# New written-out orders for the four compute engines in the third stage of a decoder kernel

## The reference, cut to what matters

```python
x = x + experts(...)                       # the last addition of layer 0
x = x + windowed_attention(layernorm(x))   # 16 heads of 16, 4 key heads, rotary angles, a sink
x = x + attention_over_heads(layernorm(x), ctx)   # per token: 16 heads against 16 heads
# gated feed-forward with a low-rank modulation taken from one more attention
z = layernorm(x); attn = causal_attention(rmsnorm(z))
mod = 0.1 * tanh(attn @ A); h = rmsnorm(z)
gate = silu(h @ W_in.T + mod * (h @ A) @ B)
x = x + z + (gate * (h @ W_up.T)) @ W_down.T
```

## Time and profile before

| | us |
|---|---|
| three runs | 3188.6, 3181.32, 3175.71 (median 3181.32) |
| the profiled execution | 3189.76, its span 3187.0 |
| mean granted clock of TensorE in it | 0.942 |
| third stage in it | about 2050 to 3187 |
| rounds in which all letters work | about 2234 to 2995 |

### The profile page before, as it was taken

The page is one execution under the profiler, slowest core; times in us unless marked ns, Lnnn a source line. Parts: engine busy times, 40 slices in busy tenths (PEclk is TensorE's granted clock), DMA queues, the critical chain, the costliest instruction groups (busy, mean ns, idle before and its releaser), DMA issues. The chain is left out here.

```text
span 3187.0 us, 68763 instructions
## 1 busy us (share of the span) xinstructions
PE 2848.2 (89%) x21832; PEld 2312.8 (73%) x21864; DVE 2618.5 (82%) x5725; ACT 1953.1 (61%) x4213; POOL 2128.5 (67%) x2555
## 2 busy tenths in 40 slices
PE   6999999999999999997786799657899989999988
PEld 3888888888888888885443577435677777777767
DVE  6888888888888888886698566478999999999973
ACT  5888878777877878784332333245565656565542
POOL 5986666666666666665576200169999999999880
PEclk8999999999999999998887799767999999999989
DMA  4564444444444444443321222300000000000000
GB/s 144 174 205 148 143 146 128 145 136 138 142 139 131 151 128 136 147 139 119 104 86 62 85 77 77 122 14 17 20 18 26 18 26 18 26 18 26 19 5 10
DMA packets 178644, 288.04 MB, mean 90 GB/s; under 512 B 42256, under 2 KB 103833, under 8 KB 177708
## 3 DMA queue, kind: packets, MB, share of 16 engines
q1 hardware_dynamic: 172206, 267.46, 26.1%
q0 software_dynamic: 6144, 16.79, 1.6%
HBM read 221.99 MB, written 53.78 MB: 87 GB/s over the span
## 5 line engine op out<-in xcount | busy, mean ns | idle before, releaser
L1747 POOL TENSOR_TENSOR l_prod<-l_sco,l_kv 128x256 f32<-128x256 f32 x512 | 444.8, 908 | 41.1 <-DVE l_sco L2259 41.1
L1740 POOL TENSOR_TENSOR l_prod<-l_q,l_kv 128x256 f32<-128x256 f32 x512 | 358.8, 741 | 17.9 <-DVE l_att L2267 17.9
L717 DVE SCALAR_TENSOR_TENSOR a_cq<-a_PQ,a_taps,a_cq 128x504 f32<-128x504 f32 (+2 forms) x384 | 281.8, 734 | 74.2 <-ACT a_cq L583 65.1
L717 DVE SCALAR_TENSOR_TENSOR a_ck<-a_PK,a_taps,a_ck 128x504 f32<-128x504 f32 (+2 forms) x384 | 280.8, 731 | 10.0 <-ACT a_ck L583 0.9
L341 POOL TENSOR_TENSOR a_tq<-a_cq,a_tq 128x512 f32<-128x512 f32 x128 | 165.9, 1296 | 132.2 <-ACT a_tq L589 132.1
L328 POOL TENSOR_TENSOR a_hrs<-a_hve,a_neghalf 128x8 f32<-128x8 f32 x128 | 209.7, 1638 | 25.6 <-DVE a_hve L734 25.1
L484 PE MATMUL a_Y<-a_wo,a_og_parts 128*128 128x256 f32 x1536 | 206.2, 284 | 4.2 <-POOL a_og_parts L335 4.2
L411 PEld LDWEIGHTS a_X<-a_wv,a_xb 128*128 128x128 f32 x1536 | 199.9, 188 | 12.1 <-issue 1.2
L411 PE MATMUL a_PQ<-a_x_hi,a_wqk 128*128 (+1 forms) x512 | 195.6, 423 | 12.5 <-issue 11.8
L341 POOL TENSOR_TENSOR a_tk<-a_ck,a_tk 128x512 f32<-128x512 f32 x128 | 163.6, 1278 | 63.3 <-ACT a_tk L589 63.3
L411 PE MATMUL a_X<-a_wv,a_xb 128*128 128x256 f32 x1536 | 204.2, 282 | 0.8 <-DMA a_xb<-a_x_lo 0.8
(11 more groups left out here) (403 smaller groups left out, 8624.9 us busy)
## 6 DMA issues: line engine op xcount, KB each, us to landing
a_wqk<-qk_parts SPq DMA_DIRECT2D x112, 512.0 KB, 3.3
a_wv<-v_parts SPq DMA_DIRECT2D x56, 512.0 KB, 3.8
a_wg<-g_parts SPq DMA_DIRECT2D x112, 256.0 KB, 3.3
a_wo<-o_parts SPq DMA_DIRECT2D x112, 256.0 KB, 2.9
a_dr<-decays SPq DMA_DIRECT2D x256, 64.0 KB, 2.5
m_hs<-sorted_rows SPq DMA_DIRECT2D x72, 128.0 KB, 2.0
sorted_outs<-m_ys SPq DMA_DIRECT2D x72, 128.0 KB, 1.7
qk_parts<-a_wqk SPq DMA_DIRECT2D x16, 512.0 KB, 3.1
```

The lines of the kernel that those rows point to most:

```text
L717: nc.vector.scalar_tensor_tensor(out=acc, in0=src, scalar=taps[p][:, tap + k:tap + k + 1], in1=acc, op0=ALU.mult, op1=ALU.add).then_inc(s_ ...
L1740: nc.gpsimd.tensor_tensor(out=prod[:, h], in0=qv[:, h:h + 1, :].to_broadcast([P, H, HD]), in1=kk, op=ALU.mult).then_inc(S("E_pqk"), 1)
L1747: nc.gpsimd.tensor_tensor(out=prod[:, h], in0=sco[:, h:h + 1, :].to_broadcast([P, HD, H]), in1=vv, op=ALU.mult).then_inc(S("E_pav"), 1)
```

## The change

The order of the pieces is new on TensorE, ScalarE, VectorE and (one swap) GpSimd, in the third stage alone. SyncE's list is the same. No instruction is added, removed or altered, and the waits inside each piece are the same. Against its neighbours:

- TensorE: `e_xT` goes to the head of the round, `d_oT` and `d_wo` from behind `m_half(1)` to just behind `e_q`, `m_half(1)` from behind `f_zT` to behind `ft_av`, `d_s` before `f_v`, `d_v` behind `ft_a`.
- VectorE: `d_x` from behind the statistics of D to right behind `combine`, `m_hidden(0)` behind `d_x`, `f_x2lo` to just ahead of the last `et_values`, `ft_gm_lo` ahead of `arguments("D")`, other orders among the `et_scores` and the `et_values`, `split_low` before `et_x`.
- ScalarE: the copies follow TensorE's new order; `exponentials("F")` comes before the copies of D, `m_tanh(0)` behind `et_exp`, `normalise("E")` to the end of the round.
- GpSimd: the `power` of E before that of D.

```diff
--- before.py
+++ after.py
@@ -1760,7 +1760,7 @@
                                                  bass.IndirectOffsetOnAxis(ap=of_tile[:, k:k + 1], axis=0)).then_inc(S(f"G_in{k}"), 16)
 
             pool.wait_ge(S("const"), 16)
-            iterate(pool, [("F", power("F", 2)), ("Et", products_av), ("Dn", power("D", 1)), ("En", power("E", 1)), ("E", products_qk),
+            iterate(pool, [("F", power("F", 2)), ("Et", products_av), ("En", power("E", 1)), ("Dn", power("D", 1)), ("E", products_qk),
                            ("G", gather)])
 
         @block.tensor
@@ -1980,9 +1980,9 @@
                 last = product(MI[:, m * R:(m + 1) * R], lambda c: fwo[:, c, m * P:(m + 1) * P], lambda c: fa[:, c, :])
             last.then_inc(S("woa_p"), 1)
             pe.wait_ge(S("woa"), 1)
-            iterate(pe, [("M", m_half(0)), ("D", d_xT), ("E", e_xT), ("Dt", d_eT), ("D", d_qk), ("Dt", d_av), ("Ft", ft_eT), ("E", e_q),
-                         ("F", f_zT), ("M", m_half(1)), ("Ft", ft_av), ("Dt", d_oT), ("D", d_qkT), ("Dt", d_wo), ("F", f_qk),
-                         ("Ft", ft_oT), ("D", d_v), ("F", f_v), ("Ft", ft_a), ("D", d_s), ("Md", m_down), ("Et", et_aT), ("Et", et_wo),
+            iterate(pe, [("E", e_xT), ("M", m_half(0)), ("D", d_xT), ("Dt", d_eT), ("D", d_qk), ("Dt", d_av), ("Ft", ft_eT), ("E", e_q),
+                         ("Dt", d_oT), ("F", f_zT), ("Dt", d_wo), ("D", d_qkT), ("F", f_qk), ("Ft", ft_av), ("M", m_half(1)),
+                         ("Ft", ft_oT), ("D", d_s), ("F", f_v), ("Ft", ft_a), ("D", d_v), ("Md", m_down), ("Et", et_aT), ("Et", et_wo),
                          ("F", f_s)])
 
         @block.scalar
@@ -2139,14 +2139,14 @@
             act.wait_ge(S("woa_p"), 1)
             nc.scalar.activation(woa[:], MI[:, 0:DC * R].rearrange("p (c r) -> p c r", c=DC), ACT.Copy).then_inc(S("woa"), 1)
             act.wait_ge(S("const"), 16)
-            iterate(act, [("M", m_tanh(0)), ("D", leave(xT["D"], EB, "D_xTp", "D_pv", "D_xT")), ("Dt", weights_T("D", "F", -4)),
-                          ("Ft", exponentials("F")), ("E", leave(xTE, P1, "E_xTp", "E_qp", "E_xT")), ("Et", et_exp),
-                          ("F", normalise("F")), ("F", f_x2), ("F", f_x1), ("Ft", weights_T("F", "D", 5)), ("E", e_q), ("F", f_x2hi),
-                          ("M", m_tanh(1)), ("Dt", leave(oT["D"], EB, "D_oTp", "D_wo", "D_oT")), ("D", spread_keys("D", P1, "D_qkTp")),
-                          ("D", queries("D", P1, "D_qkTp", "D_q")), ("Ft", leave(oT["F"], MI, "F_oTp", "F_ap", "F_oT")),
-                          ("F", f_residual), ("F", spread_keys("F", P0, "F_pj")), ("Ft", ft_mod), ("D", d_vb), ("Ft", ft_gm_hi),
-                          ("En", normalise("E")), ("Et", leave(attT, EB, "E_aTp", "E_wo", "E_aT")),
-                          ("F", queries("F", P0, "F_pj", "F_qk")), ("Dn", normalise("D")), ("F", f_vb), ("Et", split_high),
+            iterate(act, [("E", leave(xTE, P1, "E_xTp", "E_qp", "E_xT")), ("Ft", exponentials("F")),
+                          ("D", leave(xT["D"], EB, "D_xTp", "D_pv", "D_xT")), ("Dt", weights_T("D", "F", -4)), ("Et", et_exp),
+                          ("M", m_tanh(0)), ("F", normalise("F")), ("E", e_q), ("Dt", leave(oT["D"], EB, "D_oTp", "D_wo", "D_oT")),
+                          ("F", f_x1), ("Ft", weights_T("F", "D", 5)), ("D", queries("D", P1, "D_qkTp", "D_q")), ("F", f_x2),
+                          ("D", spread_keys("D", P1, "D_qkTp")), ("F", queries("F", P0, "F_pj", "F_qk")),
+                          ("F", spread_keys("F", P0, "F_pj")), ("M", m_tanh(1)), ("Ft", leave(oT["F"], MI, "F_oTp", "F_ap", "F_oT")),
+                          ("F", f_residual), ("F", f_x2hi), ("Ft", ft_mod), ("Ft", ft_gm_hi), ("D", d_vb), ("Dn", normalise("D")),
+                          ("Et", leave(attT, EB, "E_aTp", "E_wo", "E_aT")), ("F", f_vb), ("Et", split_high), ("En", normalise("E")),
                           ("D", exponentials("D"))])
 
         @block.vector
@@ -2317,12 +2317,13 @@
 
             dve.wait_ge(S("d_in"), 16 * D_WEIGHTS)
             dve.wait_ge(S("const"), 16)
-            iterate(dve, [("Et", et_scores(0)), ("Ft", arguments("F")), ("F", statistics("F", "E_x", 1)), ("Et", et_scores(2)),
-                          ("Et", et_scores(1)), ("Et", et_scores(3)), ("Et", et_shift), ("Dt", divide("D", EB)), ("Et", et_weights),
-                          ("M", m_hidden(0)), ("D", d_rope), ("Dn", combine), ("Et", et_values(0)), ("Ft", divide("F", MI)),
-                          ("Dn", statistics("D", "G_x", 2)), ("F", f_x2lo), ("Dt", d_x), ("M", m_hidden(1)),
-                          ("En", statistics("E", "D_x", 1)), ("Et", et_values(2)), ("Et", et_values(1)), ("Ft", ft_gm),
-                          ("Et", et_values(3)), ("D", arguments("D")), ("Ft", ft_gm_lo), ("Md", m_x), ("Et", et_x), ("Et", split_low)])
+            iterate(dve, [("Et", et_scores(0)), ("Ft", arguments("F")), ("Et", et_scores(1)), ("Et", et_scores(2)),
+                          ("F", statistics("F", "E_x", 1)), ("Et", et_scores(3)), ("Et", et_shift), ("Dt", divide("D", EB)),
+                          ("Et", et_weights), ("D", d_rope), ("Dn", combine), ("Dt", d_x), ("M", m_hidden(0)),
+                          ("En", statistics("E", "D_x", 1)), ("Dn", statistics("D", "G_x", 2)), ("Ft", divide("F", MI)),
+                          ("Et", et_values(1)), ("M", m_hidden(1)), ("Et", et_values(2)), ("Et", et_values(0)), ("Ft", ft_gm),
+                          ("F", f_x2lo), ("Et", et_values(3)), ("Ft", ft_gm_lo), ("D", arguments("D")), ("Md", m_x), ("Et", split_low),
+                          ("Et", et_x)])
 
 
 def decoder(nc, a, x_in, out):
```

## The result

The changed kernel takes 3249.52 us (median of 4 runs, 3239.06 to 3256.48), the kernel before 3178.93 beside it (4 runs). The ratio is 1.0211, 95% interval [1.0183, 1.0239]: slower by 2.1%, outside the range. The profiled execution took 3249.72 us. Medians here are over all runs of a kernel; the ratios leave out runs that were disturbed as a whole.

A forecast was written before the change was run, and what follows sets the result against it. VectorE's list was taken to bound the kernel at 31.54 us a round. Terms +8.4 + 2.4 + 3.2 - 5.0 + 1.1 = +10.1 us, carried to the 3181.3 us median, gave 3191 us, range 3166 to 3209.

The forecast's parts named there:

- VectorE's order alone: VectorE's list in the third stage: only L2195 gets shorter, -0.22 us a round if VectorE stays the bound.
- term of the drain: Last round of `et_values`: `f_x2lo`, 5.81 us beside GpSimd's products, no longer holds up `m_hidden(1)`; -5.0 us.
- `arguments("D")` to `arguments("F")`: `f_s` starts 0.84 us later: no cost in full rounds, with 0.3 to spare; +2.4 us in the fill.
- `divide("D")` to `ft_gm`: Chain through TensorE grows to 14.71 us; VectorE waits 0.6 us a round, net 0.35 taken, +8.4 us over 24 rounds.
- L2195: VectorE instruction directly behind `et_weights`: 643 ns at the median before, expected near its least value, 424 ns.
- The fill and the drain: Ends of the stage: fill +2.4 us, drain -5.0 and +1.1 us, with L2289 under 1.5 us.
- The lowered clock: TensorE's time lost to the clock: half of 13.7 us reaches the end, +3.2 us; bounds -3.6 to +10.1.
- rival B: TensorE's clock falls behind several short stops in nearly every round: +27 us, 3208 us, granted clock under 0.96; chance 0.20.

The follow-up runs named there:

- e6: Kernel before with `ft_gm_lo` moved ahead of `arguments("D")`, nothing else; 3231.04 us, ratio 1.0162.
- e1: Changed kernel with `ft_gm_lo` put back behind `arguments("D")`; 3245.87 us, ratio 1.0179.
- e3: Changed kernel without L2214, the scale applied in ScalarE's exponential instead; 3243.94 us, ratio 1.0157.
- e11: Changed kernel with one more GpSimd wait, ahead of product 12 of 16, for the value L2214 writes; 3238.90 us, ratio 1.0166.
- e10: Changed kernel, L2214 kept, with GpSimd's gathers behind `power("F")` and waiting for `D_av` from the tenth tile on; 3251.32 us.
- e4: VectorE's list of the kernel before, with the new lists of TensorE, ScalarE and GpSimd; 3326.03 us, ratio 1.0436.
- e7: e3 with GpSimd's two gathers put behind `power("F")` and waiting for `D_av`; 3194.42 us, ratio 1.0032.
- e8: Kernel before without L2214 and with the gathers behind `power("F")`, waiting for `D_av`; 3194.13 us, ratio 1.0038.
- e9: e7 with the gathers moved only from the tenth tile on, at their old place before that; 3171.46 us, ratio 0.9951.
- e12: Kernel before without L2214 and with the gathers moved from the tenth tile on; 3174.65 us, ratio 0.9960.
- e2: Changed kernel with `statistics("F")` put back directly behind `arguments("F")`, ahead of `et_scores(1)` and (2); 3256.53 us, ratio 1.0206.

## Why the prediction was wrong

*The step that failed* is in "VectorE's order alone": "The others that work from SBUF alone beside GpSimd's products (`combine`, `f_x2lo`, `ft_gm_lo`) stay beside products, so I leave their times." L2214 is of that kind, and I did not even list it. The earlier trace rows had the price, 5.81 us in place of 0.87 for one arrival in a burst of products; I took it as a term of the drain (-5.0) and not as a risk of each round. With 18 stalls and 57 us it is seven times the largest other term. No rival had it: the range's upper end came from the clock.

*What set it off* is the step "`arguments("D")` to `arguments("F")`": "in full rounds at the full clock it costs nothing, with 0.3 to spare". It had 0.1 us too little instead. The wait itself is 0.11 us a round; e6 shows that the move behind it, `ft_gm_lo` ahead of `arguments("D")`, alone brings the stalls, and e1 that they go with it. By which way it does so stays open.

*`divide("D")` to `ft_gm`*: predicted a wait of 0.6 us a round at L2278 for the tanh. It is there in 19 of the rounds, 6.8 / 19 = 0.36 us each. The waits for the two copies came as worked out (0.62 and 0.41 us, against 0.56 and 0.50).

*L2195* 424 to 427 ns in every full round, as said. A term that I left at its old value fell too: `ft_gm_lo` took 0.28 us in place of 0.80: in all 20 full rounds it now starts in the pause ahead of GpSimd's qk products, before the change in none. These two outweigh the waits: a clean round is 31.40 us, 0.14 shorter than before, where I had 0.35 longer.

*The fill and the drain*: L2289 took 1.12 us at most, as forecast, but the drain did not get shorter for it. From the 27th L2206 to the end it is 192.1 us before and 196.9 after, of which 3.4 are one long L2214: 1.3 longer, where I had 3.9 shorter (-5.0 and +1.1). What took the difference was not followed. The fill, from the first L2206 to the fifth, grew by 10.6 us, 9.1 of them in four long L2214; the other 1.5 stand against my 2.4.

*The lowered clock, rival B*: in the changed kernel 0.97, nearly unchanged; the mark of B, under 0.96, did not show. But e1, e3 and e11 show 0.92 or 0.93 and 3239 to 3246 us. The mechanism of B exists at more than twice the price I gave it (+27 against about +60), and in these three kernels it stands behind a stop of some 2 us ahead of `e_q`, made by the late signal. The several short stops I named did it in four rounds of e10. The kernel before had a late signal of some 2 us in two rounds: they are the 1.9 us of `recD` in the earlier trace rows, which I read and passed over as small.

## What to carry to other kernels

Ahead of a reordering, list every VectorE instruction that works from SBUF alone and mark which of them can meet a long unbroken row of GpSimd instructions. Price each at the rest of that row and not at its median. Where one has been seen long once, anywhere, fold it into another engine (here the activation's scale) or leave GpSimd a pause. And when removing a measured stall gives nothing back, look for a second disturbance behind it before giving up the first reason: here each had to go with the other.

## What the runs showed of the hardware

An instruction of VectorE from SBUF to SBUF that arrives in a row of GpSimd products without a pause can be kept out to the end of the row: 3.4 us, over the rest of one product and five more (L2214), 12.6 us over 16 (L2200). The Trainium skill, "SBUF — State Buffer", section "SBUF: two separate sides", has the lock that the two engines share held for one whole instruction; the measurements decide against that as a bound. Not every arrival is kept out: with VectorE's stop of 0.11 us ahead of L2206, L2214 starts 0.42 to 0.47 us into a product in both the long and the short cases, and without the stop (the kernel before, e1) it starts at the same point and is short in all 42 full rounds. In the full rounds of e4 it starts 0.3 to 0.5 us into the 11th, 12th or 13th product, all but once behind a longer stop, and is short in every one. What decides between them stays open.

TensorE's signal of a finished matmul can come 0.9 to 2.2 us late while GpSimd issues indirect DMAs (full rounds of the kernel before, e1, e3, e11), and it was 0.02 to 0.03 us in every full round of e7, e8, e9, e10 and e12, where the gathers wait for it. In the changed kernel and in e6 it was prompt although gathers were under way, and late in e2 at the same distance from them. Where it is late it comes 0.2 to 0.6 us behind the end of one of the two gathers: the second in e1, e2, e3 and e11, the first in 20 of the 22 full rounds of the kernel before. That the gathers are needed is shown; what else is needed is not.
